# Step 0 of an expert-and-shared feed-forward kernel: passes reordered, step 1's weights split in two parts, two input sums on GpSimd, ten more idle matmuls

## What is computed

```
def _gated_ffn(x, wi0, wi1, wo):
    return gelu(x @ wi0, approximate=True) * (x @ wi1) @ wo
share_out  = _gated_ffn(x, sWi0, sWi1, sWo)          # one shared network
expert_out = _gated_ffn(x, Wi0[label], Wi1[label], Wo[label])
gate_in = concatenate([expert_out[:, 0], share_out[:, 0]])
w = softmax(relu(gate_in @ g0) @ g1)
out = x + expert_out * w[:, 0] + share_out * w[:, 1]
```

## Time and profile before

| | us |
|---|---|
| median of 3 runs | 1979.04 (1978.45 to 1979.51) |
| the profiled execution, whole time | 1979.53 |
| its span, first to last instruction | 1977.8 |

### The profile page before, as it was taken

The page is one execution under the profiler, slowest core; times in us unless marked ns, Lnnn a source line. Parts: engine busy times, 40 slices in busy tenths (PEclk is TensorE's granted clock), DMA queues, the critical chain, the costliest instruction groups (busy, mean ns, idle before and its releaser), DMA issues.

```text
span 1977.8 us, 29016 instructions
## 1 busy us (share of the span) xinstructions
PE 1960.9 (99%) x11158; PEld 1730.2 (87%) x11158; DVE 1525.3 (77%) x1819; ACT 1036.5 (52%) x1370; POOL 80.0 (4%) x56
## 2 busy tenths in 40 slices
PE   8999999999999999999999999999999999999997
PEld 7988888899998888889999888889999988888997
DVE  7777667789887666778988767668898976676886
ACT  5554344466566444446666644344666664444463
POOL 0010000002000000000101000000010100000000
PEclk9999999999999999999999999999999999999999
DMA  5431111244453111124445311112444531111342
GB/s 158 139 108 54 49 58 49 64 144 161 139 172 96 54 59 48 54 85 140 157 145 163 96 48 54 54 54 91 150 144 139 160 96 45 63 49 48 110 158 86
DMA packets 152412, 194.83 MB, mean 99 GB/s; under 512 B 10450, under 2 KB 116946, under 8 KB 150482
## 3 DMA queue, kind: packets, MB, share of 16 engines
q1 hardware_dynamic: 152274, 192.98, 31.0%
HBM read 184.55 MB, written 8.39 MB: 98 GB/s over the span
## 4 chain that ended last, share of the span: by engine, by line
PE 97%; DVE 1%; issue 0%; ACT 0%; DMA 0%; SPq 0%; POOL 0%; DVEq 0%; POOLq 0%; ACTq 0%
PE ps_out L415 35%; PE ps_pv L396 18%; PE ps_pv L406 17%; PE ps_c L396 14%; PE ps_c L406 13%; DMA a_src<-experts 0%; DVE al L808 0%; SPq L270 0%; ACT ah L586 0%; DVE a_src L827 0%; DVE s_out L1129 0%; SPq L279 0%; DVE xl L808 0%; DVE a_src L823 0%; DVE act L904 0%
## 5 line engine op out<-in xcount | busy, mean ns | idle before, releaser
L808 DVE TENSOR_TENSOR al<-a_src,ah 128x512 fp32r<-128x512 f32 (+2 forms) x289 | 401.1, 1389 | 39.0 <-ACT ah L586 35.2
L586 ACT CAST ah<-a_src 128x2048 fp32r<-128x2048 f32 (+2 forms) x285 | 336.7, 1193 | 3.2 <-DVE a_src L827 3.2
L396 PE MATMUL ps_pv<-xh,al 128*128 128x256 f32 x1024 | 290.0, 283 | 0.2 <-DVE act L940 0.2
L396 PE MATMUL ps_pv<-xl,ah 128*128 128x256 f32 x1024 | 289.8, 283 | 0.0
L396 PE MATMUL ps_pv<-xh,ah 128*128 128x256 f32 x1024 | 289.8, 283 | 0.0
L630 ACT ACTIVATE act<-ps_c 128x256 f32<-128x256 f32 (+1 forms) x192 | 87.5, 456 | 311.5 <-PE ps_c L396 174.2
L396 PE MATMUL ps_c<-xh,al 128*128 128x256 f32 x772 | 219.1, 284 | 3.8 <-DVE al L808 3.8
L396 PE MATMUL ps_c<-xl,ah 128*128 128x256 f32 x772 | 219.1, 284 | 0.0
L396 PE MATMUL ps_c<-xh,ah 128*128 128x256 f32 x772 | 219.0, 284 | 0.0
L685 ACT COPY ps_pv<-ps_c 128x512 f32<-128x512 f32 x127 | 72.5, 571 | 269.7 <-PE ps_c L406 182.1
L415 PE MATMUL ps_out<-wo0h,hidl 128*128 128x512 f32 x512 | 199.7, 390 | 0.8 <-DVE wo0l L808 0.8
(11 more groups left out here) (95 smaller groups left out, 3916.4 us busy)
## 6 DMA issues: line engine op xcount, KB each, us to landing
a_src<-experts SPq DMA_DIRECT2D x256, 256.0 KB, 3.8
raw_wo<-experts SPq DMA_DIRECT2D x128, 256.0 KB, 2.8
a_src<-shared SPq DMA_DIRECT2D x128, 256.0 KB, 3.0
g_sb<-g_rows SPq DMA_DIRECT2D x16, 1024.0 KB, 5.4
raw_wo<-shared SPq DMA_DIRECT2D x64, 256.0 KB, 2.8
x_src<-x_cols SPq DMA_DIRECT2D x32, 256.0 KB, 3.9
g_sb<-x_rows SPq DMA_DIRECT2D x7, 1024.0 KB, 4.9
out<-s_out SPq DMA_DIRECT2D x7, 1024.0 KB, 7.0
```

What stands on the lines that cost most here:

```text
L396: mm = nc.tensor.matmul(ps[:, a * HALF:(a + 1) * HALF], a_op[ap][:, i, a, k, :], x_op[xp][:, j, k, h, :], start=(start and a == 0 and k == ...
L586: nc.scalar.copy(a_op[HI][:, i:j, :, :, :], a_src[m % 2][:, i:j, :, :, :]).then_inc(a_hi_done, 1)
L808: nc.vector.tensor_tensor(to, of, hi.bitcast(F32), ALU.subtract).then_inc(done, 1)
```

## The change

Four parts, all in step 0 and in the operands of step 1:

- The first six products of step 0 are made by `direct`, which goes pass by pass over the whole product (4 matmuls a pass) and waits before each pass only for the half that it needs: hi by hi first, then the passes with lo parts.
- The first group of step 1's weights (four blocks) is split into hi and lo in two parts of two blocks, with sums, splits and input lo parts interleaved in a new order on VectorE. All later counts of `a_hi_done` and `a_ready` are one higher. `c11_product(0)` is behind these instructions now.
- The input differences P7 and P4 (T3 and T4) are made by GpSimd.
- 20 idle matmuls take the place of 10.

```diff
-IDLE_MATMULS = 10
+IDLE_MATMULS = 20
 def a_splits(m, g):
-    return 4 if m == 0 else m * 3 + (g + 2)
+    return 4 if m == 0 else m * 3 + (g + 3)
@@ TensorE @@
+            def direct(i, j, ps, start, order):
+                for q, (ap, xp, ready) in enumerate(order):
+                    for done, count in ready:
+                        pe.wait_ge(done, count)
+                    for a in (GATE, LIN):
+                        for k in range(2):
+                            mm = nc.tensor.matmul(ps[:, a * HALF:(a + 1) * HALF], a_op[ap][:, i, a, k, :],
+                                                  x_op[xp][:, j, k, 0, :],
+                                                  start=(start and q == 0 and a == 0 and k == 0),
+                                                  stop=(q == 2 and a == 1 and k == 1), skip_group_check=True)
+                return mm
             def first_step():
-                pe.wait_ge(a_ready, 1)
-                pe.wait_ge(x_ready, 1)
-                product(P1, P1, 0, ps_c11, True)
-                pe.wait_ge(a_ready, 2)
-                pe.wait_ge(x_ready, 2)
-                product(P2, P2, 0, ps_c11, False).then_inc(direct_done, 1)
+                direct(P1, P1, ps_c11, True, [(HI, HI, [(a_hi_done, 1), (x_hi_done, 1)]), (HI, LO, [(x_ready, 1)]),
+                                              (LO, HI, [(a_ready, 1)])])
+                direct(P2, P2, ps_c11, False, [(HI, HI, [(a_hi_done, 2), (x_hi_done, 2)]), (HI, LO, [(x_ready, 2)]),
+                                               (LO, HI, [(a_ready, 2)])]).then_inc(direct_done, 1)
-                pe.wait_ge(x_ready, 3)
-                product(P1, P7, 0, ps_p5, True)
-                pe.wait_ge(x_ready, 4)
-                product(P2, P3, 0, ps_p5, False).then_inc(direct_done, 1)
-                pe.wait_ge(a_ready, 3)
-                product(P7, P1, 0, ps_c21, True)
-                pe.wait_ge(a_ready, 4)
-                product(P4, P2, 0, ps_c21, False).then_inc(direct_done, 1)
+                direct(P1, P7, ps_p5, True, [(HI, HI, [(x_hi_done, 3)]), (LO, HI, []), (HI, LO, [(x_ready, 3)])])
+                direct(P2, P3, ps_p5, False, [(HI, HI, [(x_hi_done, 4)]), (LO, HI, []), (HI, LO, [(x_ready, 4)])]
+                       ).then_inc(direct_done, 1)
+                direct(P7, P1, ps_c21, True, [(HI, HI, [(a_hi_done, 3)]), (HI, LO, []), (LO, HI, [(a_ready, 3)])])
+                direct(P4, P2, ps_c21, False, [(HI, HI, [(a_hi_done, 4)]), (HI, LO, []), (LO, HI, [(a_ready, 4)])]
+                       ).then_inc(direct_done, 1)
...
                 def operands(i):
                     if i in (P1, P7, P4):
-                        pe.wait_ge(a_ready, a_splits(n, (P1, P7, P4).index(i)))
+                        pe.wait_ge(a_ready, 5 if n == 1 and i == P1 else a_splits(n, (P1, P7, P4).index(i)))
+                    if n == 1 and i == P6:
+                        pe.wait_ge(a_ready, a_splits(1, 0))
@@ ScalarE @@
+            def second_a_hi(i):
+                sc.wait_ge(direct_done, 2)
+                sc.wait_ge(sums_done, i // 2 + 1)
+                nc.scalar.copy(a_op[HI][:, i:i + 2, :, :, :], a_src[1][:, i:i + 2, :, :, :]).then_inc(a_hi_done, 1)
             def first_step():
...
-                a_hi(1, 0)
+                second_a_hi(P5)
+                second_a_hi(P6)
             def expert_step(n, c, b):
...
-                    sc.wait_ge(x_sums_done, 4)
+                    sc.wait_ge(x_sums_done, 3)
                     nc.scalar.copy(x_op[HI][:, P7, :, 0, :], x_src[:, P7, :, :]).then_inc(x_hi_done, 1)
...
                 if n == 1:
+                    sc.wait_ge(x_sums_done, 4)
                     first_x_hi(P4)
@@ VectorE, first_step @@
                 difference(P6, P3, P5)
-                for i in range(3):
-                    weight_sums(1, i)
+                first_x_lo(P5, 5)
+                weight_sums(1, 0)
+                weight_sums(1, 1)
+                second_a_lo(P5, 5)
+                first_x_lo(P6, 6)
+                second_a_lo(P6, 6)
+                weight_sums(1, 2)
                 c11_product(0)
-                a_lo(1, 0)
-                first_x_lo(P5, 5)
-                first_x_lo(P6, 6)
                 dve.wait_ge(gelu_done, 2)
                 nc.vector.tensor_tensor(act[:, LIN, :, HALF:TOK], act[:, GATE, :, HALF:TOK], ps_pv[:, :, HALF:2 * HALF],
                                         ALU.mult).then_inc(product_done, 1)
-                dve.wait_ge(x_sums_done, 2)
-                difference(P4, P2, P6)
-                difference(P7, P3, P7)
                 first_x_lo(P7, 7)
                 a_lo(1, 1)
@@ GpSimd, ahead of everything else it does @@
+            pool.wait_ge(x_ready, 3)
+            pool.wait_ge(x_sums_done, 2)
+            difference(P7, P3, P7)
+            difference(P4, P2, P6)
```

More of the change, by code:

```diff
@@ L579, in a_hi @@
                 if m == 1:
-                    sc.wait_ge(direct_done, 2 if g == 0 else 4)
+                    sc.wait_ge(direct_done, 4)
                 else:
@@ L846, in first_a_lo, with second_a_lo @@
                 lo(a_op[LO][:, i, :, :, :], a_src[0][:, i, :, :, :], a_op[HI][:, i, :, :, :], a_ready)
+            def second_a_lo(i, count):
+                dve.wait_ge(a_hi_done, count)
+                lo(a_op[LO][:, i:i + 2, :, :, :], a_src[1][:, i:i + 2, :, :, :], a_op[HI][:, i:i + 2, :, :, :], a_ready)
             def first_x_lo(i, count):
```

## The result

The changed kernel takes 1981.65 us in the median of 20 runs (1980.59 to 1983.03), the kernel before 1978.84 us beside it (1978.43 to 1980.1, 20 runs). The ratio is 1.0014 with a 95% interval of 1.0008 to 1.0020: 2.8 us slower. That is inside the 0.2% that I had counted as no change, though the interval leaves a ratio of 1 out. The forecast was 1982.2 us, that is +3.2. The profiled execution took 1982.25 us with a span of 1979.4 us.

A forecast was written before the change was run, and what follows sets the result against it. It took step 2's start on TensorE as the bound: +2.2 (P1 later) - 0.4 (stall before P5 gone) + 1.4 (half clock) = +3.2 us on the median 1979.04, forecast 1982.2 us, range 1980.2 to 1983.5.

The forecast's parts named there:

- What bounds the kernel: Whole kernel: TensorE runs without a stop from step 2, so the change is worth what it moves step 2's start.
- Passes and idle matmuls: Step 0 on TensorE: starts between 7.5 and 9.2, ends between 19.1 and 20.8; both edits cost nothing, covered by waiting.
- The order on VectorE: VectorE before step 1's P1: `c11_product(0)` now stands last, so P1 would start at 22.0 against 21.92.
- GpSimd's differences: Two differences on GpSimd take turns with VectorE's lo part and first sum: +2.1 us, P1 at 24.1.
- The clock: TensorE from step 1's P1: after three to five us idle it runs at 1.2 GHz for 3.15 us, +1.4 us.
- The sum: At step 2's start and the end: +2.2 (P1 later) - 0.4 (stall before P5 gone) + 1.4 (half clock) = +3.2 us.
- Rival (a): Clock stays low over all of P1 and P5 and beyond: 1983.0 to 1983.5 us, chance 0.17.
- Rival (b): TensorE's clock does not fall before P1, or rises at once: +1.8, 1980.8 us, chance 0.06.
- Rival (c): GpSimd and VectorE don't meet: P1 at 22.0, stall gone, 1978.7 us, chance 0.05.
- Rival (d): Step 0's earlier end counts in full, P1 at 19.4: faster by over 0.2%, chance 0.02.

The follow-up runs named there:

- the reordered kernel: Changed kernel with GpSimd idle, `c11_product(0)` early and later VectorE and ScalarE work reordered: 1975.10 us, ratio to the kernel before 0.9979.
- the second profile of before: The kernel before, unchanged, profiled once more: 1978.32 us (1 run), its input differences starting at 12.28 and step 2 at 38.40.

## Why the prediction was right

**What bounds the kernel.** Right for the span: its differences are in the start of step 2, as the table shows for each variant. Some 0.4 to 0.7 us of the measured +2.8 is not in the span, which the prediction did not consider.

**Passes and idle matmuls.** Right in their size to half a us. Step 0 started at 7.65 and its last matmul at 19.15, inside 7.5 to 9.2 and 19.1 to 20.8, the idle ones took 6.57 us, and in the median the two parts alone are worth 0.45 us, which can't be told from none. "Nothing" was a little too strict: the profile that I read had late weights, which made the cover thicker than in the other one. There P1 starts 20.85 - 12.28 = 8.57 us behind the differences and not 7.93, since it follows step 0.

**The order on VectorE.** Right. The releaser of P1 is L905, and moving that one instruction changes the time by 2.8 us. This is the step that a reader of the change is most likely to miss, since the wait that matters (`product_done` 1) is in no line of the diff.

**GpSimd's differences.** Right: +2.1 expected, 1.13 + 1.10 = 2.2 measured, and gone when the same instructions run at another time. The sentence of the Trainium skill on two SBUF inputs ("SBUF — State Buffer", "Who interferes with whom") agrees with these runs by the 1.82 and 1.78 us against 0.69 and 0.68. A product with one input in PSUM says the same less strongly: `c11_product(0)` kept its 0.41 us when it ran at the start of GpSimd's stretch (14.04 in the run with the early `c11_product(0)`), though that one overlapped it for 0.2 us only.

**The clock.** Right in kind and size: 1.4 expected, 1.30 measured over P1 and P5 against the run with 16 more matmuls. In the profile the low stretch covered P1.

**The sum.** From the start of the differences to ScalarE's save of P5 it is 27.42 - 12.63 = 14.79 us. Before it was 25.52 - 13.99 = 11.53 in the first profile, which I had read, and 24.22 - 12.28 = 11.94 in the second: +3.26 and +2.85, where the sum says +3.2. Behind the difference between the two is mostly the term that I put at nothing, the end of step 0. Absolute times missed by 1.1 to 1.3 us (P1 at 24.1 expected, 22.98 measured; step 2 at 42.9 and 41.59). The term behind that is the landing of the weight blocks ahead of the differences, which I took from one profile; the differences began 1.4 us earlier in that of the changed kernel. So the fit of +3.26 to +3.2 is partly luck in which profile I had read. Over all runs it is +2.8, and 2.1 to 2.4 in the span.

**Rivals.** Rival (a), slower by over 0.2%, needed the low clock over P1 and P5; it ended after P1. Rival (b), a clock that does not fall, is what the run with 16 more matmuls made: 1980.09, and I had put it at 1980.8. Rival (c), no meeting with GpSimd, is what the run with the held-back differences made: 1977.91, and I had put it at 1978.7. Both were off by 0.7 to 0.8 us in the same direction. The passes and idle matmuls at nothing fit that, with their 0.45 us; the rest stays open. Rival (d), faster by over 0.2%, asked for `c11_product(0)` ahead of the lo parts and doubted that this would do: that edit alone made 1978.89, and only the reordered kernel came that far.

## What to carry to other kernels

Before a step is fed earlier, list every count that its first instruction waits for and find where each is raised in the new order: the split made one of P1's two conditions ready early and moved the other behind seven instructions. Ask of work given to a second engine what the first one does at that moment: here each 0.6 us difference given to GpSimd cost VectorE about 1.1 us where VectorE's next instruction read two inputs from SBUF, and both together cost it 0.3 to 0.4 us (0.95 and 1.12 in place of 0.69) in a stretch where it was mostly idle. And an idle stretch of TensorE has a price twice, once as the wait and once as the slow work behind it, so a few matmuls on zeros in an unavoidable gap are worth trying (here 1.30 us).

## What the runs showed of the hardware that was not expected

The low clock lasts for different times, as the prediction had expected, and does not always end soon after work begins. In the kernel before, it was low for 3.15 us of work. In the run with GpSimd's differences alone it was low from the first product on for 6 us of unbroken work; in the second profile of before, step 0 began at full clock and fell to half 1.1 us into its work, after the same ten idle matmuls. Stretches of the former, then of the latter:

```profile
7.73:8.54 0.81, 0.00 (x0) 0.00 (x0) 0.74 (x2) 0.81 (x3) 0.00 (x0) 0.50 1.04 283
8.54:14.50 5.96, 5.96 (x28) 5.96 (x29) 5.33 (x9) 4.45 (x8) 0.44 (x1) 0.50 1.04 350
14.60:18.00 3.40, 3.40 (x31) 3.40 (x30) 3.37 (x2) 0.88 (x2) 2.44 (x2) 1.00 0.90 299
```

```profile
7.75:8.85 1.10, 1.10 (x9) 1.10 (x10) 1.10 (x2) 0.65 (x2) 0.00 (x0) 1.00 0.92 271
8.90:12.25 3.35, 3.35 (x18) 3.35 (x17) 2.64 (x4) 2.63 (x5) 0.00 (x0) 0.50 1.01 333
```

28 matmuls in 5.96 us are 0.213 each, where 31 in 3.40 us are 0.11 to 0.12. At 0.09 us a matmul the 28 slow ones are 2.5 us, by which step 0 of such an execution ends later. So a change at the start of a kernel should be read from more than one profile.

The change itself has a share in this. From 8 to 14 us, nearly all of it in step 0, the mean granted clock is 0.72, 0.72 and 0.50 in the three profiles with ten of them (the kernel before twice, GpSimd's differences alone) and 1.00 in all seven profiles with twenty and the new passes, which no run separates. The idle stretch ahead of step 0 is 2.1 to 3.5 us in the three and at most 0.84 in the seven. In the changed kernel this gain is mostly covered by the wait for P1.

In the first 4 us of a profile the granted clock reads 1.00 while the idle matmuls of 512 columns follow each other at 0.4 us, the pace of 512 columns at 1.2 GHz (ten in 4.03 us). Two stretches of the changed kernel, the second with step 0's first matmuls in it:

```profile
1.20:5.40 4.20, 4.20 (x10) 1.47 (x11) 0.40 (x1) 1.43 (x2) 0.00 (x0) 1.00 0.58 178
5.50:8.00 2.50, 2.50 (x14) 1.17 (x13) 0.57 (x2) 1.02 (x2) 0.00 (x0) 1.00 0.89 282
```

Both read 1.00, and only the second goes at twice the pace. At the start the column can't be relied on; the pace can. In the kernel before, no matmul ran between 5.46 and 8.03, so nothing there confirms the 1.00 that the prediction took from the earlier trace rows.
